# A prologue for the feed-forward stage of an adaptive-layer-norm transformer block with routed experts

## The chip, the core and the metric

The kernel runs on one core of a Trainium2 chip. The core has TensorE (PE), VectorE (DVE), ScalarE (ACT) and GpSimd (POOL), each with an instruction stream of its own, and SyncE (SP), which here issues transfers. Engines wait for one another through semaphores. An engine takes its instructions in the order in which they stand, so an instruction that waits holds up everything behind it. The metric is the device time of one execution in microseconds, the median of several.

## The reference

Input x has 16 batches of 256 tokens with 128 features. A conditioning vector per batch gives shift, scale and gate for two halves.

```
h = layernorm(x) * (1 + ca) + sa                 # per batch
n = rms(h) * ln1_w;  q, k, v = n@Wq, n@Wk, n@Wv  # 16 heads of 8, q and k normalised
p = softmax((q k^T + rel_bias[bucket]) * scale, strictly causal)
y = (p v) @ Wo + h
x = x + ga * (relu((rms(y) * ln2_w) @ W1) @ W2 + y)      # W1 128x512, W2 512x128
h = layernorm(x) * (1 + cb) + sb
s = sigmoid(h @ gate_w^T)                        # 32 experts
ids = top4(s + e_bias);  w = s[ids] / sum(s[ids])
x = x + gb * sum over the 4 experts e of w_e * ((silu(h@w1_e) * (h@w3_e)) @ w2_e)
```

All is float32.

## The kernel before

The kernel passes through four stages. A batch is two tiles of 128 tokens.

**Attention.** A loop over batches. For each of them PE makes scores for 8 units of two heads, DVE adds the bias (L1289), ACT takes the exponential (L703), PE multiplies by the values (`products`, L954). The last steps of batch b lie inside the sequence of batch b + 1: ACT brings the context out of PSUM (`context`, L710), PE transposes it (`ctx_T`, L970), DVE divides by the sum (`normalize`, L1308 and L1310), PE transposes and multiplies by Wo (`yn_T`, `y_out`), and DVE adds h and takes the statistics of y (`y_rows`, L1316 and L1320). For batch 15 these steps stand alone at the end.

**Feed-forward and routing.** The order is written by hand, engine by engine, as turns (`all_turns` and the four functions `turn`). Turn k does for a pair of batches the products of the feed-forward, for the pair before it the residual and the router's logits, and for the pair before that the choice of experts. So turns 0 and 1 fill this pipeline, turns 3 to 6 are a loop, and turns 8 and 9 drain it. The steps of one batch are:

- ACT copies y from the batch store (`stage`, L763), PE transposes it (`m_transposes`, L1040), ACT brings it out (`m_evac`, L767), PE makes the 512 hidden values (`hidden`, L1046), ACT applies relu (`relu`, L771), PE makes the second product (`mlp_out`, L1058).
- DVE scales that by the root of the RMS norm, adds y and x and takes statistics (`mlp_out` on DVE, L1477 to L1488). After a pair it takes their mean and root in 18 small instructions (`group_stats`, L324 to L1502).
- ACT normalises (`normal`, L780), DVE modulates (`modulated`, L1510 and L1512), PE transposes and makes the logits (`logits`, L1065 and L1069), ACT takes the tanh that gives the sigmoid (`routed`, L786 and L788) and copies the rows for the scatter (`copies`).
- DVE picks the four experts (`pick`, L1523 to L1553), PE counts the ranks (`ranks`, L1076), DVE makes the rows' positions (`place`, L1563 to L1569).
- POOL scatters the rows of the batch to HBM by 8 indirect transfers (L637), once the positions and the copies are there. Batches are scattered in order, through four sets of buffers. ACT's `normal` of batch b waits until the rows of batch b - 4 have been scattered.

Ahead of turn 0 DVE works out the roots for the RMS norm of all 32 tiles (L324 to L312, 18 instructions). After the last positions PE and DVE total the counts, SP writes 32 blocks of padding rows to HBM (L425), and waits for all scatters and for the padding before it loads the first sorted rows (L438).

**Experts.** 40 steps of four tiles of sorted rows, and then the sum over each token's four experts, the last stage.

## Time and profile before

| | |
|---|---|
| median of 3 runs | 689.37 us (688.49 to 689.84) |
| the profiled execution | 688.63 us, of which the span is 686.7 us |
| attention | to about 262 us of the span |
| feed-forward and routing | to 470.8 us, where the last scatter leaves POOL |
| experts and sum | from 472.4 us, the first load of sorted rows |
| busy, share of the span | PE 70%, DVE 66%, POOL 57%, ACT 46% |
| mean granted clock of PE | 0.862 |

The shares are means over stages with different limits. In the middle stage DVE is busy for 8 of every 10 us and POOL for 7 to 8, while PE has 2.4 to 8. A row of the timeline gives start, duration, engine, line, operation and operands, and in brackets how long the engine was idle before and what released it.

### The profile page before, as it was taken

The numbers are of one execution on the slowest core, as the hardware profiler recorded it, in microseconds if no ns is written. First come the engines' busy times: TensorE is split into PE (matmuls) and PEld (weight loads), VectorE is DVE, ScalarE is ACT, GpSimd is POOL, SyncE is SP. The second block draws the span as 40 slices with busy tenths as digits, with TensorE's granted clock in tenths as the row PEclk, the third lists the DMA queues.
The fourth block names the chain that finished last, engine by engine and source line by source line (L and its number), as shares of the span: only waits on it lengthen the run. The fifth ranks groups of instructions, "written<-read, shape, count | busy, mean of one in ns | idle before, by whom it ended". The sixth has DMA issues, their size and how long they took to land.

```text
span 686.7 us, 16134 instructions
## 1 busy us (share of the span) xinstructions
PE 481.4 (70%) x4426; PEld 371.9 (54%) x4427; DVE 454.3 (66%) x1486; ACT 315.2 (46%) x683; POOL 389.8 (57%) x606
## 2 busy tenths in 40 slices
PE   2568888888888776677766764222999999981057
PEld 0235555555555554565545553211899889980046
DVE  5776888888887774477786778850466666662028
ACT  0346777777787763432333323301566556430000
POOL 5565666666665400047676767773277777777700
PEclk9968999999999999977877876555999999995569
DMA  7996000000006006001111111145354545421178
GB/s 204 297 261 165 3 0 0 0 0 0 0 1 247 2 1 184 1 30 57 53 55 51 53 53 56 62 134 150 102 149 128 148 128 148 127 85 50 53 305 314
DMA packets 68850, 66.26 MB, mean 96 GB/s; under 512 B 8912, under 2 KB 60336, under 8 KB 68800
## 3 DMA queue, kind: packets, MB, share of 16 engines
q1 hardware_dynamic: 52096, 43.64, 21.5%
q0 software_dynamic: 8192, 17.84, 7.4%
q10 hardware_dynamic: 8512, 4.20, 2.1%
q8 instruction: 21, 0.34, 0.2%
q14 instruction: 29, 0.24, 0.1%
HBM read 40.86 MB, written 27.93 MB: 100 GB/s over the span
## 4 chain that ended last, share of the span: by engine, by line
DVE 26%; PE 25%; issue 22%; POOL 10%; DVEq 6%; ACT 6%; DMA 3%; POOLq 1%; SPq 1%; ACTq 0%
DVE L L1289 6%; PE PS L1046 5%; POOL xs L637 4%; POOL ys L655 3%; PE PS L931 3%; DVE yidx L1678 3%; PE PS L1137 2%; PE PS L1058 2%; PE PS L1206 2%; PE PS L906 2%; DVEq L335 2%; DVE YQ L1676 1%; PE PS L954 1%; POOL QKR L535 1%; PE PS L1069 1%
## 5 line engine op out<-in xcount | busy, mean ns | idle before, releaser
L637 POOL DMA_INDIRECT xs<-YQ,posi x128 | 124.9, 976 | 109.3 <-issue 98.3
L655 POOL DMA_INDIRECT ys<-YQ,yidx x128 | 122.6, 958 | 60.6 <-issue 34.2
L1289 DVE TENSOR_TENSOR L<-PS,BIAS 128x768 f32<-128x768 f32 x128 | 116.6, 952 | 39.0 <-PE PS L934 33.3
L703 ACT ACTIVATE PR<-L 128x768 f32<-128x768 f32 x128 | 106.0, 842 | 60.7 <-DVE L L1289 58.6
L1676 DVE SCALAR_TENSOR_TENSOR YQ<-PS,tag,YQ 128x128 f32 x160 | 56.2, 351 | 46.1 <-DVE yidx L1678 29.7
L1137 PE MATMUL PS<-BIAS,V 128*128 x320 | 64.1, 346 | 3.7 <-issue 1.6
L931 PE MATMUL PS<-YQ 32*128 32x256 f32 x512 | 47.3, 439 | 27.2 <-DVE L L1289 25.7
L1137 PEld LDWEIGHTS PS<-BIAS,V 128*128 128x128 f32 x320 | 53.0, 196 | 10.8 <-issue 10.8
L1046 PE MATMUL PS<-YT,w1s 128*128 128x256 f32 x128 | 42.3, 487 | 15.8 <-ACT YT L767 15.8
L1058 PE MATMUL PS<-w2s,hid 128*128 128x128 f32 x256 | 36.3, 300 | 14.5 <-ACT hid L771 14.5
L931 PEld LDWEIGHTS PS<-YQ 32*128 32x128 f32 x512 | 20.9, 188 | 46.8 <-DVE L L1289 33.1
L817 ACT ACTIVATE L<-PS 128x384 f32<-128x384 f32 x40 | 19.6, 491 | 54.9 <-PE PS L1137 53.6
L1206 PE MATMUL PS<-BIAS,ident 128*128 128x256 f32 x64 | 17.2, 424 | 39.3 <-DMA BIAS<-ys 38.9
L1058 PEld LDWEIGHTS PS<-w2s,hid 128*128 128x128 f32 x256 | 33.1, 209 | 19.2 <-ACT hid L771 17.9
L1046 PEld LDWEIGHTS PS<-YT,w1s 128*128 128x128 f32 x128 | 29.5, 242 | 25.2 <-ACT YT L767 20.4
L954 PE MATMUL PS<-PR,V 128*32 128x256 f32 x512 | 42.1, 400 | 1.4 <-DVE YQ L1316 1.1
L830 ACT ACTIVATE V<-PS 128x512 f32<-128x512 f32 x40 | 23.9, 597 | 33.2 <-PE PS L1129 33.2
L1129 PE MATMUL PS<-ident,PR 128*128 128x128 f32 x160 | 25.0, 281 | 18.3 <-DMA PR<-xs 18.3
L1206 PEld LDWEIGHTS PS<-BIAS,ident 128*128 128x128 f32 x64 | 13.2, 213 | 42.9 <-issue 40.9
L771 ACT ACTIVATE hid<-PS 128x1024 f32<-128x1024 f32 x16 | 16.4, 1023 | 43.7 <-PE PS L1046 43.7
L578 POOL TENSOR_SCALAR V<-RAW,rs 128x128 f32<-128x128 f32 x32 | 23.7, 749 | 22.1 <-issue 7.3
L906 PE MATMUL PS<-wqkv,hT 128*128 128x384 f32 x64 | 29.8, 596 | 6.6 <-DVE YQ L1276 4.3
(256 smaller groups left out, 1114.2 us busy)
## 6 DMA issues: line engine op xcount, KB each, us to landing
PR<-xs SPq DMA_DIRECT2D x160, 72.0 KB
BIAS<-ys SPq DMA_DIRECT2D x12, 512.0 KB, 8.2
modb<-mod_rows SPq DMA_DIRECT2D x1, 4096.0 KB, 14.0
dist_rep<-dist_row SPq DMA_DIRECT2D x4, 768.0 KB, 7.8
xs<-pad_row SPq DMA_DIRECT2D x33, 72.0 KB, 12.4
xs<-pad_row SPq DMA_DIRECT2D x1, 2304.0 KB, 17.8
X<-in_x ACTq DMA_DIRECT2D x4, 512.0 KB, 6.6
BIAS<-dist_rep SPq DMA_DIRECT2D x4, 512.0 KB, 8.6
```

The costliest lines, as they stand in the source:

```text
L637: pool.indirect_dma_start(out=xs, out_offset=bass.IndirectOffsetOnAxis(ap=posi[j][:, t * TOPK + k:t * TOPK + k + 1], axis=0), in_=ROWS[j][ ...
L655: pool.indirect_dma_start(out=ys, out_offset=bass.IndirectOffsetOnAxis(ap=yidx[:, n:n + 1], axis=0), in_=YQ[:, n * D:(n + 1) * D], in_offs ...
L703: act.activation(PR[u % 4][:, :], L[u % 2][:, :], ACT.Exp).then_inc(s["exp_done"], 1)
L906: last = pe.matmul(bank(PRE + t, 3 * D), hT[par][:, t * P:(t + 1) * P], wqkv[:, :], start=True, stop=True)
L931: pe.matmul(bank(S_A + quad, SEQ), KT[par][r, 0:P], QM[par][r, j, :], start=True, stop=True)
L954: pe.matmul(o, V[par][:, 0, h, :], pr[:, (j % 2) * HW:(j % 2) * HW + SEQ], start=True, stop=False, skip_group_check=True)
L1046: last = pe.matmul(bank(1 + ch // 2, SEQ, (ch % 2) * SEQ), w1s[:, ch * P:(ch + 1) * P], mT[n % 2], start=True, stop=True)
L1058: last = pe.matmul(bank(3 + 4 * (n % 2), P, t * P), hid[n % 2][:, ch, t * P:(t + 1) * P], w2s[:, ch, :], start=(ch == 0), stop=(ch == HID ...
L1137: last = pe.matmul(bank(2 + 2 * par + j // 2, 2 * INNER, (j % 2) * 2 * INNER), xgT[par][:, j * P:(j + 1) * P], w13[:, bass.ds(e * (2 * INN ...
L1206: last = pe.matmul(bank(n % 4, SEQ), ident[:, :], G[r][:, :, k, :], start=(k == 0), stop=(k == TOPK - 1))
L1289: return dve.tensor_tensor(L[u % 2][:, :].rearrange("p (j w) -> p j w", j=2), PS[:, at:at + 2, 0:HW], BIAS[:, u, :].rearrange("p (j w) -> ...
L1676: dve.scalar_tensor_tensor(to, bank(6 + par, D, k * D), tag[buf][:, k, 0:1], to, ALU.mult, ALU.add)
```

## The change

The two buffers for staged y and its transpose move from the context tile YT to the two RAW tiles of the attention, which are free once the last values and the last normalised q and k are made. So ACT can stage batches 0 and 1 inside the last attention sequence. The feed-forward's turns 0 and 1, and in turn 2 the choice of experts for batches 0 and 1 (on DVE all of turn 2), are replaced by a prologue in which batches 0 to 3 are handled one by one, and whose first products stand among the last context steps. The roots of the RMS norm are taken in two parts: tiles 0 to 29 ahead of the context steps of batch 15, and the last two at the end of turn 7. The turns from 3 on keep their order, except for that second part.

```diff
--- before.py
+++ after.py
-        mT = [YT[:, 2 * i, :] for i in range(2)]
-        YS = [YT[:, 2 * i + 1, :].rearrange("p (t d) -> p t d", t=TPB) for i in range(2)]
+        raw_flat = [RAW[i][:, :, :].rearrange("p t d -> p (t d)") for i in range(2)]
+        mT = [raw_flat[i][:, 0:SEQ] for i in range(2)]
+        YS = [raw_flat[i][:, SEQ:SEQ + TPB * D].rearrange("p (t d) -> p t d", t=TPB) for i in range(2)]
...
-        def all_turns(eng, turn):
+        def all_turns(eng, turn, entered=False):
...
-                turn(pair(k), pair(k - 1), pair(k - 2), pair(k + 1), k - 1, (k - 1) // 2)
-            for k in range(3):
-                one(k)
+                turn(pair(k), pair(k - 1), pair(k - 2) if k > 2 else [], pair(k + 1), k, (k - 1) // 2)
+            if not entered:
+                one(2)
...
+            def stage(b, n):
+                act.wait_ge(s["y_ready"], b + 1)
+                if not at(b, 0, 1):
+                    act.wait_ge(s["m_t"], b - 1)
+                act.activation(YS[n % 2], tok(Y, b, 0, TPB), ACT.Copy).then_inc(s["ys_staged"], 1)
...
+                if left == 0:
+                    act.wait_ge(s["v_ready"], NB)
+                    act.wait_ge(s["qn_done"], NB)
+                    stage(0, 0)
+                    stage(1, 1)
...
-            act.wait_ge(s["o2_done"], NB)
-            stage(0, 0)
-            stage(1, 1)
+            m_evac(0, 0)
+            context(NB - 1, 1)
+            relu(0, 0)
+            yn_T(NB - 1)
+            stage(2, 2)
+            m_evac(1, 1)
+            stage(3, 3)
+            normal(0, 0, 0, 0)
+            relu(1, 1)
+            routed(0, 0)
+            copies(0, 0)
+            m_evac(2, 2)
+            relu(2, 2)
+            m_evac(3, 3)
+            normal(1, 1, 1, 0)
+            routed(1, 1)
+            relu(3, 3)
+            copies(1, 1)
+            stage(4, 0)
+            stage(5, 1)
             all_turns(act, turn)
...
-            products(NB - 1, 1, 3)
-            ctx_T(NB - 1)
-            yn_T(NB - 1)
-            y_out(NB - 1)
-
-
-            pe.wait_ge(s["l_ready"], NB * UNITS + 2)
-            pe.wait_ge(s["w1_scaled"], 1)
...
+            pe.wait_ge(s["l_ready"], NB * UNITS + 1)
+            m_transposes(0, 0)
+            products(NB - 1, 1, 3)
+            pe.wait_ge(s["l_ready"], NB * UNITS + 2)
+            pe.wait_ge(s["w1_scaled"], 1)
+            hidden(0, 0)
+            ctx_T(NB - 1)
+            mlp_out(0, 0)
+            yn_T(NB - 1)
+            y_out(NB - 1)
+            m_transposes(1, 1)
+            hidden(1, 1)
+            logits(0, 0)
+            mlp_out(1, 1)
+            ranks(0, 0)
+            m_transposes(2, 2)
+            hidden(2, 2)
+            mlp_out(2, 2)
+            m_transposes(3, 3)
+            hidden(3, 3)
+            logits(1, 1)
+            mlp_out(3, 3)
+            ranks(1, 1)
             all_turns(pe, turn)
...
+            def y_roots(first, n):
+                r = slice(first, first + n)
+                mean_var(dve, st, r)
+                st.wait()
+                st(dve.tensor_tensor(st1[:, r], mean[:, r], mean[:, r], ALU.mult))
+                st.wait()
+                st(dve.scalar_tensor_tensor(var[:, r], st1[:, r], RMS_EPS, var[:, r], ALU.add, ALU.add))
+                st.wait()
+                rsqrt(dve, st, rstd[:, r], var[:, r], st1[:, r], st2[:, r])
+                st.wait()
+
+            y_roots(0, NT - TPB)
             normalize(NB - 1)
-            y_rows(NB - 1)
-
-
-            dve.wait_ge(s["y_ready"], NB)
-            mean_var(dve, st)
-            st.wait()
-            st(dve.tensor_tensor(st1[:, :], mean[:, :], mean[:, :], ALU.mult))
-            st.wait()
-            st(dve.scalar_tensor_tensor(var[:, :], st1[:, :], RMS_EPS, var[:, :], ALU.add, ALU.add))
-            st.wait()
-            rsqrt(dve, st, rstd[:, :], var[:, :], st1[:, :], st2[:, :])
-            st.wait()
             dve.wait_ge(s["ld_mod"], 16)
+            dve.wait_ge(s["h_scaled"], NB)
...
-                    group_stats(k, 2 * TPB)
+                    group_stats(k, 0, 2 * TPB)
...
+                if at(k, NPAIR - 1):
+                    y_roots(NT - TPB, TPB)
+
+            mlp_out(0, 0, 0)
+            group_stats(0, 0, TPB)
+            y_rows(NB - 1)
+            modulated(0, 0)
+            pick(0, 0)
+            place(0, 0)
+            mlp_out(1, 1, 1)
+            group_stats(1, TPB, TPB)
+            modulated(1, 1)
+            mlp_out(2, 2, 0)
+            pick(1, 1)
+            place(1, 1)
+            mlp_out(3, 3, 1)
+            group_stats(2, 0, 2 * TPB)
+            modulated(2, 2)
+            modulated(3, 3)
+            all_turns(dve, turn, entered=True)
```

POOL and SP keep their rows. **PE at the end of attention**, from the last products of batch 15. L954/L973 and L959/L978 are the products with the values, L970/L989 the transposes of the context, L976/L995 and L983/L1002 those of the normalised context and the product with Wo, L1040/L1050 the transposes of staged y, L1046/L1056 the hidden products, L1058/L1068 the second products. Before:

```order
L954 MATMUL PS<-PR,V 32x256 x4
L959 MATMUL PS<-PR,V 32x128 x4
L954 MATMUL PS<-PR,V 32x256 x4
L959 MATMUL PS<-PR,V 32x128 x4
L970 MATMUL PS<-ident,YT 128x128 x8
L976 MATMUL PS<-ident,YN 128x128 x2
L983 MATMUL PS<-wo,YNT 128x128 x2
L1040 MATMUL PS<-ident,YT 128x128 x2
L1046 MATMUL PS<-YT,w1s 128x256 x4
L1058 MATMUL PS<-w2s,hid 128x128 x8
```

After:

```order
L973 MATMUL PS<-PR,V 32x256 x4
L978 MATMUL PS<-PR,V 32x128 x4
L1050 MATMUL PS<-ident,RAW 128x128 x2
L973 MATMUL PS<-PR,V 32x256 x4
L978 MATMUL PS<-PR,V 32x128 x4
L1056 MATMUL PS<-RAW,w1s 128x256 x4
L989 MATMUL PS<-ident,YT 128x128 x8
L1068 MATMUL PS<-w2s,hid 128x128 x8
L995 MATMUL PS<-ident,YN 128x128 x2
L1002 MATMUL PS<-wo,YNT 128x128 x2
L1050 MATMUL PS<-ident,RAW 128x128 x2
L1056 MATMUL PS<-RAW,w1s 128x256 x4
```

The transposes and the hidden products of batch 0 now stand ahead of the context transposes, the second product of batch 0 ahead of those of the normalised context.

**DVE at the same place**, from the division of batch 15 on. Before, y and the statistics of batch 15 follow at once, then the roots of 32 tiles and the residuals of two batches:

```order
L1308 RECIPROCAL rden<-PS 128x32
L1310 TENSOR_TENSOR YN<-PS,rden 128x256
L1316 TENSOR_TENSOR YQ<-PS,YQ 128x256
L1320 BN_STATS stats<-YQ 128x6 x2
L324 TENSOR_TENSOR st<-stats 128x32
L325 TENSOR_TENSOR st<-stats 128x32
```

After, the roots of 30 tiles stand ahead of the division, and behind it the residual of batch 0 (L1511 to L1522) and its `group_stats`, which ends with nmr_g; then come y of batch 15, the modulation of batch 0 and its pick:

```order
L1537 SCALAR_TENSOR_TENSOR nmr_g<-mean_g,rstd_g 128x2
L1349 TENSOR_TENSOR YQ<-PS,YQ 128x256
L1353 BN_STATS stats<-YQ 128x6 x2
L1545 TENSOR_TENSOR YQ<-YQ,modb 128x2x128
L1547 TENSOR_TENSOR YQ<-YQ,modb 128x2x128
L1558 TENSOR_SCALAR score<-th 128x64
L1560 TENSOR_TENSOR sel<-score,ebias 128x64
L1564 MAX top<-sel 128x8 x2
```

Batch 0 is carried to its pick before the residual of batch 1 is taken.

**DVE at the end of turn 7**, from the positions of batch 11 on. Before, the pick of batch 12 follows the modulation of batch 13:

```order
L1567 TENSOR_REDUCE rk<-OHT 128x8
L1569 SCALAR_TENSOR_TENSOR posi<-nt,rk 128x8
L1510 TENSOR_TENSOR YQ<-YQ,modb 128x2x128
L1512 TENSOR_TENSOR YQ<-YQ,modb 128x2x128
L1523 TENSOR_SCALAR score<-th 128x64
L1525 TENSOR_TENSOR sel<-score,ebias 128x64
```

After, the 18 instructions of the second `y_roots` stand between them:

```order
L1604 SCALAR_TENSOR_TENSOR posi<-nt,rk 128x8
L1545 TENSOR_TENSOR YQ<-YQ,modb 128x2x128
L1547 TENSOR_TENSOR YQ<-YQ,modb 128x2x128
L325 TENSOR_TENSOR st<-stats 128x2
L326 TENSOR_TENSOR st<-stats 128x2
L327 TENSOR_TENSOR rstd<-stats 128x2
L329 TENSOR_SCALAR mean<-st 128x2
```

## Rows read from the trace of the kernel before

**Rows 1.** The page's costliest groups: line, engine, operation, count; busy, mean ns; idle before

```profile
L637 POOL DMA_INDIRECT xs<-YQ,posi x128 | 124.9, 976 | 109.3 <-issue 98.3
```

**Rows 2.** Waits between 297 and 471 us: who for whom, us, times, longest

```profile
POOL xs L637 <- DVE posi L1569: 10.9, 11, 1.3
```

**Rows 3.** Timeline of POOL (start, duration, engine, line, operation; idle before, releaser)

```profile
299.07 1.20 POOL L637 DMA_INDIRECT xs<-YQ,posi  x1 [62.49 <-issue]
...
420.11 0.95 POOL L637 DMA_INDIRECT xs<-YQ,posi  x1 [0.78 <-DVE posi L1569]
...
440.53 0.96 POOL L637 DMA_INDIRECT xs<-YQ,posi  x1 [0.30 <-issue]
...
469.81 0.96 POOL L637 DMA_INDIRECT xs<-YQ,posi  x1 [0.30 <-issue]
```

**Rows 4.** Timeline of DVE, the instruction that finishes a batch's positions

```profile
319.27 0.17 DVE L1569 SCALAR_TENSOR_TENSOR posi<-nt,rk 128x8 int32<-128x8 f32 x1
...
419.10 0.17 DVE L1569 SCALAR_TENSOR_TENSOR posi<-nt,rk 128x8 int32<-128x8 f32 x1
...
438.73 0.17 DVE L1569 SCALAR_TENSOR_TENSOR posi<-nt,rk 128x8 int32<-128x8 f32 x1
449.54 0.17 DVE L1569 SCALAR_TENSOR_TENSOR posi<-nt,rk 128x8 int32<-128x8 f32 x1
```

**Rows 5.** Timeline of SP's queue after the routing, and its waits there

```profile
451.68 18.68 SPq L425 DMA_DIRECT2D xs<-pad_row  x32
472.39 27.49 SPq L438 DMA_DIRECT2D PR<-xs  x40
...
SPq L442 <- DMA xs<-YQ,posi: 0.4, 1, 0.4
```

**Rows 6.** Timeline of DVE at the attention's end

```profile
261.92 0.36 DVE L1308 RECIPROCAL rden<-PS 128x32 f32<-128x32 f32 x1 [3.03 <-PE PS L970]
```

**Rows 7.** Timeline of all engines, the steps of the first batches

```profile
264.25 0.38 PE L1040 MATMUL PS<-ident,YT 128*128 128x128 f32 x2
265.11 1.99 PE L1046 MATMUL PS<-YT,w1s 128*128 128x256 f32 x8 [0.47 <-ACT YT L767]
268.22 2.05 PE L1058 MATMUL PS<-w2s,hid 128*128 128x128 f32 x16 [1.11 <-ACT hid L771]
270.43 0.61 DVE L1477 SCALAR_TENSOR_TENSOR XH<-PS,rstd,YQ 128x128 f32<-128x128 f32 x2 [1.22 <-PE PS L1058]
276.23 0.61 DVE L1477 SCALAR_TENSOR_TENSOR XH<-PS,rstd,YQ 128x128 f32<-128x128 f32 x2 [3.64 <-PE PS L1058]
278.42 0.17 DVE L324 TENSOR_TENSOR tg<-stats 128x4 f32<-128x4 f32 x1
281.41 0.16 DVE L1502 SCALAR_TENSOR_TENSOR nmr_g<-mean_g,rstd_g 128x4 f32<-128x4 f32 x1
285.61 1.64 ACT L780 ACTIVATE YQ<-X,nmr_g,rstd_g 128x128 f32<-128x128 f32 x4
286.51 0.43 DVE L1510 TENSOR_TENSOR YQ<-YQ,modb 128x256 f32<-128x256 f32 x1 [4.94 <-ACT YQ L780]
```

**Rows 8.** Timeline of DVE, first pick of experts and the end of turn 2

```profile
289.44 0.20 DVE L1523 TENSOR_SCALAR score<-th 128x64 f32<-128x64 f32 x1 [1.25 <-ACT th L788]
292.98 0.60 DVE L1477 SCALAR_TENSOR_TENSOR XH<-PS,rstd,YQ 128x128 f32<-128x128 f32 x2
...
309.56 0.42 DVE L1512 TENSOR_TENSOR YQ<-YQ,modb 128x256 f32<-128x256 f32 x1
```

**Rows 9.** Timeline of PE, products at the lower clock

```profile
313.83 3.78 PE L1046 MATMUL PS<-YT,w1s 128*128 128x256 f32 x8 [1.99 <-ACT YT L767]
318.80 3.77 PE L1058 MATMUL PS<-w2s,hid 128*128 128x128 f32 x16 [0.55 <-ACT hid L771]
```

**Rows 10.** A window: length, busy of the five, granted clock, DMA share, GB/s

```profile
290.00:294.00 4.00, 2.01 (x9) 1.59 (x10) 3.54 (x16) 2.15 (x6) 0.00 (x0) 0.71 0.00 0
```

**Rows 11.** Timeline of DVE, the pick of batch 12, after turn 7

```profile
420.85 0.20 DVE L1523 TENSOR_SCALAR score<-th 128x64 f32<-128x64 f32 x1 [0.79 <-ACT th L788]
```

More of the change, by code:

```diff
@@ L271, in one @@
             def one(k):
[L272 to L274 removed]
+                turn(pair(k), pair(k - 1), pair(k - 2) if k > 2 else [], pair(k + 1), k, (k - 1) // 2)
+            if not entered:
+                one(2)
             with eng.Fori(0, NPAIR // 2 - 2) as four:
                 b = four * 4
[L277 to L278 removed]
+                turn(pair_of(b + 6, 2), pair_of(b + 4, 0), pair_of(b + 2, 2), pair_of(b + 8, 0), four * 2 + 3, four + 1)
+                turn(pair_of(b + 8, 0), pair_of(b + 6, 2), pair_of(b + 4, 0), pair_of(b + 10, 2), four * 2 + 4, four + 1)
             for k in range(NPAIR - 1, NPAIR + 2):
@@ L754, in _ @@
                 sequence(NB - 1 - left, left % 2 ^ 1, left=left)
-            context(NB - 1, 1)
-            yn_T(NB - 1)
-            def stage(b, n):
-                act.wait_ge(s["y_ready"], b + 1)
-                if not at(b, 0, 1):
-                    act.wait_ge(s["m_t"], b - 1)
-                act.activation(YS[n % 2], tok(Y, b, 0, TPB), ACT.Copy).then_inc(s["ys_staged"], 1)
             def m_evac(b, n):
@@ L1590, in turn @@
                     modulated(*rows[1])
-            all_turns(dve, turn)
+                if at(k, NPAIR - 1):
[17 more added lines that the diff above has]
+            all_turns(dve, turn, entered=True)
             dve.wait_ge(s["cnt_pe"], 1)
```

30 lines of the change are left out of this document (14 added, 16 removed).

## The prediction

> **What bounds the kernel now.** I read the page first. Its slices show three regimes, and the change touches the seam between the first two and the order at the start of the second. The costliest group is POOL's scatter: 128 of them at a mean of 976 ns [rows 1]. So the first question is whether POOL sets the length of the middle stage. The timeline of POOL says that it runs from 299.07 to 470.77 [rows 3], 171.7 us. The last 24 scatters take 470.77 - 440.53 = 30.24 us, 1.26 us each, so 128 of them without a pause would take 161.5. The table of waits gives the difference: 11 times in this stage POOL waited for a batch's positions from DVE, 10.9 us in all [rows 2]. The last of these waits is at batch 11, whose positions are done at 419.27 [rows 4] and whose first scatter starts at 420.11 [rows 3], 0.84 us later. From there POOL has no more pause. So the chain that ends the stage is: DVE's turns up to the positions of batch 11, and then 40 scatters of POOL. An earlier first scatter alone is worth nothing; an earlier DVE is worth what it brings at batch 11, as long as the batches behind it keep up.
>
> A second chain ends close behind. After the last positions, at 449.71 [rows 4], SP is released and writes the padding from 451.68 to 470.36. It then reads its tables, and stood before its wait for the scatters 0.4 us before the last of them landed; the first load went out at 472.39 [rows 5]. So if the scatters ended earlier and the padding did not, only 0.4 us would be gained.
>
> **The start of the stage, before.** At the end of attention DVE waits 3.03 us for the context transposes, until 261.92 [rows 6]. The first residual starts at 270.43, the second at 276.23, after a wait of 3.64 us for PE; its statistics end at 281.57, and then DVE waits 4.94 us until 286.51, because ACT takes its normalisation, at 285.61, only behind the relus of batches 2 and 3 [rows 7]. The first pick starts at 289.44 [rows 8]. The pipeline is entered when the modulation of batch 3 ends, at 309.98 [rows 8]; the loop starts there.
>
> **The steps of a batch.** Durations at the full clock, all from [rows 7] and [rows 8]. Transposes of y and their copy out: 265.11 - 264.25 = 0.86. Hidden products 1.99. Relu with its hops 268.22 - 267.10 = 1.12. Second products 2.05. A round of all this on PE takes 5.8 (276.23 - 270.43). Residual 278.42 - 276.23 = 2.19. Statistics of a group 281.57 - 278.42 = 3.15, for 18 instructions. Normalisation 1.64 / 4 x 2 = 0.82 a batch. Modulation 0.88. From there to a usable tanh 289.44 - 287.39 = 2.05. Pick 292.98 - 289.44 = 3.54. Positions about 1.1.
>
> **Part 1, the first products among the context steps.** PE's transposes of batch 0 fit ahead of the last exponential, but the hidden products stand ahead of the context transposes. These need their copy by ACT anyway, so I charge 1.99 less some 0.6: the division comes at about 263.3 and not 261.9. Bounds are 0 (all beside the copy) and 1.99. The first roots of 30 tiles, 18 instructions like those of the group statistics, so at least 3.15 us, lie in DVE's wait of 3.03 + 1.4; if the wait were gone, they would cost these 3 us, as they do now behind the statistics of batch 15. In return the residual of batch 0 needs hidden products from about 260.1 (the context transposes' place: 261.92 less a copy and eight transposes, estimated 1.8), 1.99 + 1.12 + 2.05, so it starts at 265.4 and not 270.43. ACT's two staging copies lie in its idle time before an exponential, and the two RAW tiles have no reader left. I take both as free.
>
> **Part 2, batches 0 to 3 one by one.** I follow the engines' orders by hand.
> - DVE: residual and statistics of batch 0 to 270.8. ACT's normalisation to 271.6, y of batch 15 beside it, modulation to 272.7, tanh 274.8, pick to 278.3, positions 279.4. The first scatter could leave at 280.4, 18.6 us earlier than now.
> - Then residual 1 and its own statistics (a second run of 18 instructions, 3.15 us that did not exist) to 284.8, normalisation and modulation 286.5, residual 2 to 288.7, pick 1 to 292.2, positions 293.3, residual 3 and statistics to 298.6.
> - PE is behind this, not ahead: the relu of batch 3 stands on ACT behind the tanh of batch 1 (288.6), so it ends at 289.6, the second products of batch 3 at 291.7, ranks of batch 1 to 292.3. Only then come the transposes of batch 4. Batch 5's relu ends at 292.3 + 0.86 + 5.8 + 1.99 + 1.1 = 302.1, and ACT has the normalisation of batches 2 and 3 behind it. So DVE waits from 298.6 to 303.0, and the modulation of batch 3 ends at 303.0 + 0.8 + 0.88 = 304.7.
>
> That is 5.3 us earlier than 309.98. I take 4.7 at the positions of batch 2 (now 319.27, [rows 4]), since the clock's falls lie otherwise and the first tanh of the loop comes late. Bounds: 6 with PE at its full clock throughout, 3 with one batch more at the lower one (hidden products 3.78 for 1.99, second ones 3.77 for 2.05 [rows 9], 3.5 a batch, part of it in waits). The loop is the same code on all engines, and DVE bounds it, so 4.7 arrives at batch 11. The 18.6 us at the first scatter do not: they become POOL's pauses at batches 1 and 2.
>
> **Part 3, the second roots.** They are 18 more small instructions at the end of turn 7. The nearest row is the group statistics, 3.15 us [rows 7]. DVE waits 0.79 us for the tanh of batch 12 at this place [rows 11], so 2.4 reach the pick. Bounds: 3.15, if the tanh comes no later, and 1.5. The positions of batches 12 to 15 are thus earlier by only 4.7 - 2.4 = 2.3. Those of batch 13, at 438.90 [rows 4], would be at 436.6, and 0.84 later, at 437.4, its scatters can start, now 440.53 [rows 3]. POOL is then without pause again. So the last scatter is 3.1 earlier.
>
> **Part 4, the padding.** The last positions are 2.3 earlier, and so are SP's 18.68 us of padding. SP has lost 0.4 of waiting at most, so the first load is at 472.39 - 2.3 - 0.4 = 469.7. By the scatters it would be 469.3. The padding becomes the last, and the stage ends 2.7 us earlier. Bounds 0.7 (loop 3 earlier, roots 2.7) and 5 (loop 6, roots 1.5, rounded up).
>
> **The sum.** Parts 1 and 2 bring -4.7 at the loop's entry, the second roots +2.4, SP's margin before the scatters' landing -0.4: -2.7. The profiled execution has a span of 686.7 and takes 688.63; 1.9 lies around the span and stays. It would become 685.9. The median is 689.37, 0.74 more, so I predict 686.7.
>
> **The clock as a rival, and the slower side.** In the window 290 to 294 the granted clock of PE fell from 1.00 to 0.50, mean 0.71, after PE had been busy for little of the stretch, 2.01 of 4 us with nine matmuls [rows 10]; there are two levels, 2.4 and 1.2 GHz. Before the change turns 0 and 1 run wholly at the upper one. In the prologue PE is more often idle, for some 3 us before the logits of batch 0 above all, so I expect one fall near 274. If the clock then stays low until batch 5's relu, batches 2 to 5 cost 3.5 us more each. PE waits for ACT or DVE for some 4 us in that stretch, so 14 - 4 = 10 us reach the loop, which enters 5 later than now, and with the second roots the stage ends 7 later: about 696. It decides from the point at which the prologue loses more than 2.7, one batch at the lower clock beyond my count. Against it: in the whole stage the page's slices show the clock fall and come back again and again, with a mean of 5 tenths only where PE has almost nothing to do, and in the prologue PE has the products of a batch every 12 us or faster. The skill speaks for it: the Trainium skill, "TensorE: Matmul & The Clock Gate", Part 1, holds that the low clock is the rule and "activity releases the throttle", so a sparse prologue would be throttled more than the dense turns that it replaces. The fall in rows 10 agrees; that the low clock lasts through the prologue no row shows. I give the slower side 0.08.
>
> **Other rivals.**
> - The gain is spent before the end (0.18). The loop enters only 2 to 3.5 earlier, the roots cost 2.4 to 3, and the padding hides the rest: 0 to 1.4 gained, 688.0 to 689.4. For it: three terms of 2 to 5 us are differenced. Against it: the order by hand leaves DVE idle for only 4.4 us before the loop, where it idles some 13 now (3.03 + 1.22 + 3.64 + 4.94).
> - The second roots are covered and the scatters decide (0.14): if the tanh of batch 12 comes later than now, or the padding lands sooner, the gain is 3.5 to 5, 684.4 to 685.9.
> - POOL was the bound all along (0.02): the 18.6 us pass through, 670.8. The 11 waits speak against it.
>
> The forecast itself, 1.4 to 3.5 gained, gets 0.58. What a measurement here can tell from no change is 0.2%, 1.4 us. Faster: 0.58 + 0.14 + 0.02 = 0.74; the same 0.18; slower 0.08. The range from 684.6 to 689.4 leaves out the slow clock, POOL and the edges of the others.
>
> **What the profile after would show.** The first scatter near 280 and a pause of POOL at batches 1 and 2; a DVE wait of about 4 us before the modulation of batch 2; the positions of batch 2 near 314.6; those of batch 11 near 414.4 and of batch 15 near 447.2; a POOL wait at batch 13; SP's first load near 469.7 with no wait for scatters. I am wrong if the positions of batch 2 are later than 317, or if the load waits for scatters that end after the padding.

## The result, and the profile after

The changed kernel takes 686.21 us (median of 5 runs, 685.09 to 687.61) where the kernel before took 689.84 in 5 runs of the same session. The ratio is 0.9951, with a 95% interval from 0.9938 to 0.9964: 3.4 us faster, with an interval of 2.5 to 4.3. The forecast was 686.7. The profiled execution took 686.9 with a span of 685.0, against 688.63 and 686.7. That pair differs by only 1.7: the profile of before was one of its quicker runs and that of after one of its slower ones.

For comparing profiles I need a common start. The last pair but one of DVE's additions to the scores is the same in all kernels, a row with a wait of 1.44 for PE. I call its start the mark. Here it is, first in the kernel before, then in the changed one:

```profile
253.04 1.82 DVE L1289 TENSOR_TENSOR L<-PS,BIAS 128x768 f32<-128x768 f32 x2 [1.44 <-PE PS L934]
```

```profile
254.02 1.82 DVE L1322 TENSOR_TENSOR L<-PS,BIAS 128x768 f32<-128x768 f32 x2 [1.44 <-PE PS L953]
```

The attention ahead of it took 1.0 us longer in that execution of the changed kernel. Over all my profiles the mark lies between 251.9 and 254.6.

DVE in the changed kernel, from the timeline (columns as in [rows 3 and 4]):

```profile
264.42 0.36 DVE L1341 RECIPROCAL rden<-PS 128x32 f32<-128x32 f32 x1 [0.83 <-PE PS L989]
266.76 0.61 DVE L1511 SCALAR_TENSOR_TENSOR XH<-PS,rstd,YQ 128x128 f32<-128x128 f32 x2 [1.52 <-PE PS L1068]
...
275.79 0.19 DVE L1558 TENSOR_SCALAR score<-th 128x64 f32<-128x64 f32 x1 [1.89 <-ACT th L790]
280.24 0.17 DVE L1604 SCALAR_TENSOR_TENSOR posi<-nt,rk 128x8 int32<-128x8 f32 x1
...
303.59 0.42 DVE L1545 TENSOR_TENSOR YQ<-YQ,modb 128x256 f32<-128x256 f32 x1 [3.62 <-ACT YQ L782]
315.09 0.17 DVE L1604 SCALAR_TENSOR_TENSOR posi<-nt,rk 128x8 int32<-128x8 f32 x1
...
405.59 0.17 DVE L1604 SCALAR_TENSOR_TENSOR posi<-nt,rk 128x8 int32<-128x8 f32 x1
416.40 0.17 DVE L1604 SCALAR_TENSOR_TENSOR posi<-nt,rk 128x8 int32<-128x8 f32 x1
427.54 0.17 DVE L1604 SCALAR_TENSOR_TENSOR posi<-nt,rk 128x8 int32<-128x8 f32 x1
...
449.12 0.17 DVE L1604 SCALAR_TENSOR_TENSOR posi<-nt,rk 128x8 int32<-128x8 f32 x1
```

Take 1.0 off each for the late mark and lay them beside [rows 4, 6, 7]: the prologue runs as it was worked out, within half a microsecond at every step. The wait of 3.62 at the modulation of batch 2 is the one that was forecast as about 4. Counted from the mark, the positions of batch 2 come at 61.07 instead of 66.23, 5.2 us earlier. But those of batch 11 are only 3.7 earlier, and those of batch 15 only 1.4.

POOL and SP at the same places (compare [rows 3, 5]); the last column of the SP rows is the number of transfers:

```profile
281.43 1.20 POOL L638 DMA_INDIRECT xs<-YQ,posi  x1 [43.87 <-issue]
295.48 0.97 POOL L638 DMA_INDIRECT xs<-YQ,posi  x1 [4.00 <-DVE posi L1604]
316.10 1.17 POOL L638 DMA_INDIRECT xs<-YQ,posi  x1 [10.79 <-DVE posi L1604]
...
428.54 0.97 POOL L638 DMA_INDIRECT xs<-YQ,posi  x1 [1.10 <-DVE posi L1604]
...
468.64 0.96 POOL L638 DMA_INDIRECT xs<-YQ,posi  x1 [0.30 <-issue]
```

```profile
451.22 18.82 SPq L426 DMA_DIRECT2D xs<-pad_row  x32
471.73 26.75 SPq L439 DMA_DIRECT2D PR<-xs  x40
```

Counted from the mark, the first scatter is 18.6 us earlier and the last only 2.2: POOL waits 26.9 us for positions now, 10.9 before [rows 2]. The padding ends last, and SP no longer waits for scatters. The first load of sorted rows goes out 217.71 behind the mark instead of 219.35, so 1.6 us of the gain are seen there in this pair of profiles. What lies outside that stretch differs from one execution to the next in any kernel: the mark by up to 2.6 us, and the time from the first load to the end of the span (214.3 before, 213.3 after) between 213.3 and 215.2.

### The profile page after: what moved, and what is told of

It reads as the page before. It is cut to its first block, busy times and chain, and to the rows that moved or that the text cites. A ratio compares the mean times of both kernels' runs of the same rounds, so it can differ in the third digit from the quotient of the medians.

```text
span 685.0 us, 16172 instructions
## 1 busy us (share of the span) xinstructions
PE 474.9 (69%) x4426; PEld 367.0 (54%) x4427; DVE 458.8 (67%) x1522; ACT 315.6 (46%) x683; POOL 390.4 (57%) x606
## 4 chain that ended last, share of the span: by engine, by line
DVE 31%; issue 24%; PE 20%; DVEq 6%; POOL 6%; ACT 6%; SPq 3%; DMA 3%; POOLq 1%; ACTq 0%
DVE L L1322 6%; PE PS L1056 4%; POOL ys L656 4%; DVE yidx L1732 3%; PE PS L950 2%; PE PS L1068 2%; PE PS L1239 2%; SPq L426 2%; DVEq L336 2%; POOL QKR L536 2%; ACT YT L711 2%; DVE YQ L1730 1%; PE PS L1170 1%; PE PS L1079 1%; DVEq L1730 1%
## 5 line engine op out<-in xcount | busy, mean ns | idle before, releaser
L1056 PE MATMUL PS<-RAW,w1s 128*128 128x256 f32 x128 | 40.4, 470 | 13.8 <-ACT RAW L769 13.8
L1068 PE MATMUL PS<-w2s,hid 128*128 128x128 f32 x256 | 34.4, 290 | 13.0 <-ACT hid L773 13.0
L973 PE MATMUL PS<-PR,V 128*32 128x256 f32 x512 | 41.7, 396 | 1.4 <-DVE YQ L1349 1.1
L1056 PEld LDWEIGHTS PS<-RAW,w1s 128*128 128x128 f32 x128 | 28.4, 234 | 22.6 <-ACT RAW L769 18.0
L1068 PEld LDWEIGHTS PS<-w2s,hid 128*128 128x128 f32 x256 | 31.3, 200 | 17.1 <-ACT hid L773 15.7
```

Source lines behind the costliest of these rows:

```text
L973: pe.matmul(o, V[par][:, 0, h, :], pr[:, (j % 2) * HW:(j % 2) * HW + SEQ], start=True, stop=False, skip_group_check=True)
L1056: last = pe.matmul(bank(1 + ch // 2, SEQ, (ch % 2) * SEQ), w1s[:, ch * P:(ch + 1) * P], mT[n % 2], start=True, stop=True)
L1068: last = pe.matmul(bank(3 + 4 * (n % 2), P, t * P), hid[n % 2][:, ch, t * P:(t + 1) * P], w2s[:, ch, :], start=(ch == 0), stop=(ch == HID ...
```

## The experiments

All are timed in five rounds beside the kernel before; ratios are to it, with 95% intervals. What settles most of them is a table worked out from the profiles: the time from the mark to the positions of batch 2 (the entry), from there to those of batch 10 (the loop), and on to those of batch 15 (the end). The first three columns come from one profile each, the ratio from all executions.

```
kernel                        entry   loop    end   ratio   (interval)
before                        66.23  89.02  41.25
staging alone                 66.22  88.94  41.27  1.0006  (0.9994 to 1.0018)
before, more roots            66.22  88.89  43.36  1.0008  (0.9996 to 1.0020)
before, written out           66.23  86.71  40.18  0.9945  (0.9925 to 0.9965)
seam alone                    62.96  88.83  40.22  0.9934  (0.9915 to 0.9953)
seam alone, written out       62.98  86.74  40.16  0.9898  (0.9878 to 0.9918)
after (the change)            61.07  90.50  43.53  0.9951  (0.9938 to 0.9964)
after, roots in the wait      60.96  88.86  40.10  0.9907  (0.9893 to 0.9922)
  the same, written out       61.10  86.54  40.58  0.9894  (0.9875 to 0.9912)
after, roots in both          63.31  88.77  43.68  0.9951  (0.9934 to 0.9968)
after, scatter held           63.47  90.39  43.53  0.9961  (0.9949 to 0.9973)
after, PE kept busy           62.39  89.88  43.55  0.9947  (0.9929 to 0.9965)
after, written out            63.97  86.51  43.35  0.9911  (0.9891 to 0.9930)
after, seam apart             69.42  89.82  43.51  1.0099  (1.0070 to 1.0128)
```

### The second roots in DVE's wait

```
             group_stats(2, 0, 2 * TPB)
+            y_roots(NT - TPB, TPB)
             modulated(2, 2)
...
-                if at(k, NPAIR - 1):
-                    y_roots(NT - TPB, TPB)
```

> The changed kernel with the second roots (18 small DVE instructions for the last two tiles) taken from the end of turn 7 and put between the statistics of batches 2 and 3 and the modulation of batch 2, where DVE waited 3.62 us. My theory (Part 3 of the prediction): the roots cost about 2.3 us in front of the pick of batch 12 and nothing in the wait. Then the modulation of batch 2 still starts at about 303.6 with no or a short wait, batches 12 to 15 are 2.3 earlier (positions of batch 15 near 446.8 instead of 449.1), the padding ends 2.3 earlier, but then the scatters decide: batch 11 starts them at about 417.3, 40 scatters take 50.4, so the first load goes out near 470.0 instead of 471.7: a gain of 1.7 us, 684.5 (683.9 to 685.3). Rival 1: the tanh of batch 12 comes late enough that turn 7 waits for it anyway: positions of batch 15 move by under 0.8, gain under 0.6. Rival 2: the roots fill more than the wait at the entry and push everything by their excess: the modulation of batch 2 starts later than 304, no gain or a loss.

Measured: 683.07, ratio 0.9907. Its DVE and SP rows:

```profile
303.16 0.42 DVE L1545 TENSOR_TENSOR YQ<-YQ,modb 128x256 f32<-128x256 f32 x1 [0.42 <-ACT YQ L782]
...
414.15 0.17 DVE L1604 SCALAR_TENSOR_TENSOR posi<-nt,rk 128x8 int32<-128x8 f32 x1
422.07 0.17 DVE L1604 SCALAR_TENSOR_TENSOR posi<-nt,rk 128x8 int32<-128x8 f32 x1
```

```profile
445.54 19.13 SPq L426 DMA_DIRECT2D xs<-pad_row  x32
467.25 32.60 SPq L439 DMA_DIRECT2D PR<-xs  x46
```

The modulation of batch 2 still waits 0.42, so the roots are free there. From batch 11 to 12 takes 7.92 us instead of 11.14: against this kernel the second roots cost 3.2 in turn 7, not the 2.3 I expected. The gain of 3 us over the changed kernel is larger than 1.7; the loop, too, is shorter, 88.86 for 90.50. Later experiments follow that.

### The roots added to the kernel before

```
                 if rows:
                     modulated(*rows[1])
+                if at(k, NPAIR - 2):
+                    y_roots(NT - TPB, TPB)
```

> The kernel before with the roots of the last two tiles worked out a second time at the end of the turn in which the changed kernel has them (18 small DVE instructions behind the modulation of batch 11). Nothing else changes. It measures Part 3 by itself. My theory: 3.15 us of instructions, less the wait of 0.79 for the tanh of batch 12 that they cover: positions of batches 12 to 15 come 2.4 later, the padding is last, 691.7 (691.1 to 692.4). Rival: the kernel with them in the wait showed 3.2 between the same two positions; if the tanh comes early whatever stands there, the cost is 3.2: 692.5 or more. Third: POOL's scatters decide the end: then 1.6 or less, since POOL had 0.8 of wait left at batch 11 only.

Measured: 690.39, ratio 1.0008. The table shows 2.1 more at the end (43.36 for 41.25). The kernel before and the one with the staging alone are the odd ones: without roots there, every other kernel takes 40.1 to 40.6 on this stretch. The tanh of batch 12 in the kernel before:

```profile
420.60 0.22 ACT L788 ACTIVATE th<-PS 128x64 f32<-128x64 f32 x1 [1.15 <-PE PS L1069]
```

ACT waited 1.15 for the logits, which PE computed at the lower clock (granted 0.50 from 418 to 420 us); in four of the five kernels with the shorter end it waits 0.72, with PE at the upper clock, and the fifth (the roots in the wait, written out) has 1.15 and the longest of those ends, 40.58. So the wait of 0.79 in [rows 11], which I took off the price, goes with PE's clock at that place. It stood in both profiles that have this order of turns and no roots there. At the first load the profile shows 1.8 us more than before (221.10 behind the mark for 219.35), because before it the scatters ended last and now the padding does. The time rose by only 0.5 us (interval -0.3 to 1.4). Where the rest went is open.

### The scatters held back

```
+            pool.wait_ge(s["pos_ready"], 2)
             with pool.Fori(0, NB // GROUP) as g:
```

> The changed kernel with one more wait on POOL: the first scatter is held until the positions of batch 1 are there, so it starts near 295.3 and not at 281.4. My theory (Part 2): the early first scatter is worth nothing, since POOL pauses 26.9 us for positions behind it; 16 scatters take 20.2, so the ones of batch 2 still start at about 316 (positions at 315.1). Time as after, 686.2 within 0.6. Rival: POOL's own length decides somewhere behind (scatters landing later in the first group hold ACT's normalisation of batches 4 and 5, or POOL is not again waiting by batch 11): 2 to 14 us slower.

Measured: 686.88, ratio 0.9961, against 0.9951: as after.

```profile
296.03 1.29 POOL L638 DMA_INDIRECT xs<-YQ,posi  x1 [60.43 <-issue]
...
327.88 0.95 POOL L638 DMA_INDIRECT xs<-YQ,posi  x1 [1.32 <-DVE posi L1605]
...
468.97 0.96 POOL L638 DMA_INDIRECT xs<-YQ,posi  x1 [0.31 <-issue]
```

The first scatter is 14.6 us later, POOL waits for positions again at batch 3, and the last scatter is 0.3 later. (Counted from the mark it is 16.6 and 2.3; the 2.3 are the longer entry in the table, 63.47 for 61.07. That goes with PE's clock and not with the hold: the modulation of batch 1, which needs no scatter, already waits 3.02 for 0.95, and kernels without the hold show the same.) The early scatters are worth nothing that the time could show.

### The staging alone

```
-            act.wait_ge(s["o2_done"], NB)
-            stage(0, 0)
-            stage(1, 1)
...
+                if left == 0:
...
+                    stage(0, 0)
+                    stage(1, 1)
```

(with the raw buffers for the staged tiles, as in the change; the rest is the kernel before)

> The kernel before with the staging alone: staged y and its transposes lie in the raw buffers and ACT copies batches 0 and 1 among the exponentials of batch 15 instead of behind the last context copy; the turns, their order and the roots are as before. My theory: the transposes of batch 0 already followed the output product of attention without a wait, so nothing is gained by the staging itself: 689.8 within 0.7 (0 to 0.3 us of PE's sequence at most). Rival: the copies among the exponentials delay the last context (slower by 0.7), or free ACT at the seam by 0.7 us and bring that (faster by 0.7).

Measured: 689.61, ratio 1.0006; the entry takes 66.22, as before. The staging is worth nothing by itself and only makes room for what follows.

### The seam undone, and the seam alone

The first puts batch 0's transposes and products back behind the last context steps in the changed kernel, on PE as shown (lines that wait are left out) and on ACT likewise:

```
-            m_transposes(0, 0)
             products(NB - 1, 1, 3)
-            hidden(0, 0)
             ctx_T(NB - 1)
-            mlp_out(0, 0)
             yn_T(NB - 1)
             y_out(NB - 1)
+            m_transposes(0, 0)
+            hidden(0, 0)
+            mlp_out(0, 0)
```

> The changed kernel with the last context steps undone from the first products on PE and ACT: products of the last context, context transposes, transposes of y, output product, and only then the transposes, hidden and second products of batch 0; on ACT both context copies ahead of the copy and relu of batch 0. DVE, the staging and the order of batches 0 to 3 stay. My theory: the division is about 1.5 earlier (262.9), but the residual of batch 0 starts at about 271.2 instead of 266.8, and since DVE is the chain of the prologue, every step up to the entry of the loop is 4 to 6 later (modulation of batch 3 ends near 310, as in the kernel before); with the second roots still in turn 7 the stage ends later than in the kernel before: 691.5 (690 to 693), slower than after by 4.5 to 6 and than before by 1.5 to 3. Rival: the gain of the change comes from handling the batches singly and not from the order at the seam: then it stays within 1.5 of after (686 to 687.7).

Measured: 694.88, ratio 1.0099: 6.8 us slower than before (4.8 to 8.8), beyond the expected band. Its rows, of DVE and of PE:

```profile
273.45 0.61 DVE L1510 SCALAR_TENSOR_TENSOR XH<-PS,rstd,YQ 128x128 f32<-128x128 f32 x2 [10.21 <-PE PS L1068]
```

```profile
264.23 1.22 PE L1002 MATMUL PS<-wo,YNT 128*128 128x128 f32 x4 [0.47 <-ACT YNT L717]
265.24 0.64 PE L1050 MATMUL PS<-ident,RAW 128*128 128x128 f32 x2
266.35 3.78 PE L1056 MATMUL PS<-RAW,w1s 128*128 128x256 f32 x8 [0.47 <-ACT RAW L769]
```

DVE stands 10.2 us before the first residual. Most of my miss there is the clock: the output product, the transposes and the hidden products of batch 0 ran at the lower level (granted 0.50 from 264 to 270 us; 3.78 where 1.99 was usual), behind two microseconds, 262 to 264, in which PE was busy for 0.47. Single handling without the seam is worse than no change.

The second is the other half: the kernel before with the staging and the seam, DVE's code as it was, the batches in pairs, all roots in one piece. On PE (waits left out; ACT likewise):

```
+            m_transposes(0, 0)
             products(NB - 1, 1, 3)
+            hidden(0, 0)
             ctx_T(NB - 1)
+            mlp_out(0, 0)
             yn_T(NB - 1)
             y_out(NB - 1)
+            m_transposes(1, 1)
+            hidden(1, 1)
+            mlp_out(1, 1)
-            all_turns(pe, turn)
+            all_turns(pe, turn, 1)
```

> The kernel before with the seam alone: raw buffers for the staging, batches 0 and 1 staged among the last exponentials, transposes and products of batch 0 among the last context steps on PE and ACT, those of batch 1 right behind the output product. DVE is as before: all roots behind the statistics of batch 15, batches handled in pairs from the first turn, no second roots. My theory: hidden products ahead of the context transposes put the division and with it the roots and residual 0 about 1.1 later (271.5), but residual 1 no longer waits for PE (273.7 instead of 276.2), the relus of batches 2 and 3 and so the first normalisation come 3.5 earlier, and the modulation of batch 3 ends near 306.3 instead of 310.0. With no second roots to pay, positions 15 are 3.5 earlier than before (446.0) and the time is about 686.0 (685.0 to 687.5), no worse than the whole change. Rival: what brings the gain is the single handling (statistics and tanh of batch 0 early); then this stays within 1.2 of before (688.1 to 689.5).

Measured: 684.99, ratio 0.9934, the level of the whole change or a little better, and a little better than I expected.

```profile
271.62 0.61 DVE L1489 SCALAR_TENSOR_TENSOR XH<-PS,rstd,YQ 128x128 f32<-128x128 f32 x2
273.82 0.61 DVE L1489 SCALAR_TENSOR_TENSOR XH<-PS,rstd,YQ 128x128 f32<-128x128 f32 x2
283.04 0.42 DVE L1522 TENSOR_TENSOR YQ<-YQ,modb 128x256 f32<-128x256 f32 x1 [3.88 <-ACT YQ L782]
...
294.40 0.17 DVE L1581 SCALAR_TENSOR_TENSOR posi<-nt,rk 128x8 int32<-128x8 f32 x1
```

Both residuals start without a wait, as expected (compare 270.43 and 276.23 in [rows 7]). The entry takes 62.96, 3.3 less than before; 1.0 more comes at the end (40.22 for 41.25), where the wait for the late tanh of batch 12 is gone. So the reordering at the seam is what pays. Handling the batches singly buys at most 2 us more at the entry and costs 3.3 at the end with the second roots in turn 7 (43.53 for 40.22). With those roots in the wait it costs nothing there, but whether it then gains can't be told: 0.9907 and 0.9934 have intervals that meet.

### A stall at the loop's jump back

In the changed kernel's trace something stood in turn 5, the second pass of DVE's loop. First ACT's tanh of batch 6, then DVE's rows around the jump:

```profile
350.32 0.22 ACT L790 ACTIVATE th<-PS 128x64 f32<-128x64 f32 x1 [1.15 <-PE PS L1079]
```

```profile
349.51 0.42 DVE L1547 TENSOR_TENSOR YQ<-YQ,modb 128x256 f32<-128x256 f32 x1
352.66 0.19 DVE L1558 TENSOR_SCALAR score<-th 128x64 f32<-128x64 f32 x1 [2.72 <-ACT th L790]
...
354.88 0.20 DVE L1569 FIND_INDEX8 topi<-top,sel 128x8 uint32<-128x32 f32 x1 [0.93 <-issue]
```

The tanh is done at 350.54, the pick starts at 352.66, and inside it DVE stands 0.93 with no releaser. With the roots in the wait it starts 0.25 behind the tanh. Two experiments write the loop of turns 3 to 6 out on DVE alone, in the changed kernel and in the one with the roots in the wait (the other engines keep the loop):

```
-            with eng.Fori(0, NPAIR // 2 - 2) as four:
+            for k in range(3, NPAIR - 1):
+                one(k)
```

> The changed kernel with DVE's loop over turns 3 to 6 written out, the other engines as they are. In the changed kernel's trace DVE started the pick of batch 6, the first instruction behind its loop's jump back, 2.1 us after its tanh was ready, and stood 0.93 more inside it with no releaser; in the kernel before it started at once. Theory: a stall of DVE's instruction supply at the jump back, 3 us, of which 0.7 to 1.5 reach the positions behind it (the rest lies in the wait for the ranks). Written out, pick 6 starts within 0.3 of its tanh, positions of batch 11 are near 415.3 and the time is 685.2 (684.2 to 686.0). Rival: the late start has to do with ACT or a semaphore and not with the jump: no change (686.2 within 0.5). Second rival: longer straight code meets the same stall at other places: same or up to 3 slower.

> The kernel with the second roots in the wait at the loop's entry, and DVE's loop written out. That kernel showed no late start at the jump back (pick 6 came 0.64 after the work before it, 0.25 after its tanh). By the theory of the stall nothing is to be gained here: 683.1 within 0.6. If the written-out code itself were faster or slower (no loop overhead, more code to bring in), it would show here as a difference of more than 0.8.

Measured: 684.13 (0.9911) and 682.92 (0.9894). The pick of batch 6 starts on time in both, but the loop also took 2.3 us less where no stall had been (86.54 for 88.86), although the time of that kernel hardly shows it (0.9894 for 0.9907, intervals that overlap). So two things were mixed, and a control on the kernel before parts them.

> The kernel before with DVE's loop written out, a control for the changed kernel with the same edit, which gained 2.7 us on it. Two causes are mixed there. From the positions of batch 2 to those of batch 10 took 89.0 us in the kernel before, 90.5 in the changed one, 88.9 with the second roots in the wait, and 86.5 in both written-out kernels. Theory: the loop form costs 2.4 us in any kernel (88.9 to 86.5), and the late start at the jump back 1.5 more, in the changed kernel alone. Then this control goes from 89.0 to 86.5 between the two positions, and is faster than before by 2 to 2.5: 687.5 (686.9 to 688.2). Rival: all of the 2.7 is the stall at the jump, and the loop form costs nothing in itself: 689.7 within 0.6.

Measured: 684.92, ratio 0.9945, and 86.71 in the loop: as the theory had it. In time 3.8 were gained, interval 2.4 to 5.2, more than the 2.0 to 2.5 expected; at the first load the profile shows 2.1 (217.25 behind the mark for 219.35), since the scatters end last there. The same residual of batch 7, first with the loop, then written out:

```profile
341.46 0.61 DVE L1477 SCALAR_TENSOR_TENSOR XH<-PS,rstd,YQ 128x128 f32<-128x128 f32 x2
342.22 0.43 DVE L1481 TENSOR_TENSOR XH<-XH,modb 128x256 f32<-128x256 f32 x1
342.77 0.43 DVE L1484 TENSOR_TENSOR X<-X,XH 128x256 f32 x1
```

```profile
342.56 0.60 DVE L1481 SCALAR_TENSOR_TENSOR XH<-PS,rstd,YQ 128x128 f32<-128x128 f32 x2
343.19 0.42 DVE L1485 TENSOR_TENSOR XH<-XH,modb 128x256 f32<-128x256 f32 x1
343.65 0.42 DVE L1488 TENSOR_TENSOR X<-X,XH 128x256 f32<-128x256 f32 x1
```

These instructions last as long, but their starts lie 0.76 and 0.55 apart with addresses from the loop's counter and 0.63 and 0.46 with fixed ones. The steps of `group_stats` behind them, whose tiles have fixed addresses in both, mostly keep their distance of 0.20; but two of them (L328 and L329) last 0.40 and 0.32 with the loop and 0.17 and 0.16 written out. So what is shown is the price of the loop's form. Addresses from the counter may be part of it, and the semaphore values waited for are made from the counter too; nothing here separates them.

The stall itself was tested by moving the loop in the code: the roots worked out twice, ahead of the loop and behind it.

```
             group_stats(2, 0, 2 * TPB)
+            y_roots(NT - TPB, TPB)
             modulated(2, 2)
```

> The changed kernel with the roots of the last two tiles worked out twice, in the wait at the loop's entry and again at the end of turn 7. The work in front of batch 12 is that of the changed kernel; what differs is that 18 instructions more stand ahead of DVE's loop. Theory of instruction supply: the late start at the jump back (2.1 and 0.9 us) depends on where the loop's code lies and not on what it does, so it goes away here as in the kernel with these roots in the wait alone: positions 2 to 10 take 88.9 and not 90.4, time 684.8 (684.0 to 685.8), and the remaining 1.7 to that kernel is the price of the roots in turn 7. Rival: the late start comes from the roots that stand behind the loop: then it stays, 686.2 within 0.7.

Measured: the loop takes 88.77 and the late start is gone, as the theory of instruction supply had it. The time, 685.95 with a ratio of 0.9951, does not show the 1.4 expected; its twelve runs spread from 683.5 to 688.6, and in the profiled one the prologue met a longer low clock (entry 63.31). The DMA view of 300 to 420 us has the last piece, the queue that brings instructions (packets, MB, share), first in the changed kernel, then in the one with the roots in the wait:

```profile
q14 instruction: 9, 0.07, 0.2%
```

```profile
q14 instruction: 4, 0.03, 0.1%
```

The four kernels with the late start (the change, scatters held, PE kept busy, seam apart) have 9 packets there; the other ten have 4 or 5. Two of the nine fall into the 5 us of the stall, 350 to 355, where the kernel with the roots in the wait has none:

```profile
q14 instruction: 2, 0.02, 1.3%
```

The Trainium skill, "Runtime: NRT & Kernel Launch", "Instruction fetch mechanics", says it: a taken branch whose target lies outside the two pages at hand makes the engine wait for a DMA of the target page. The trace agrees with it, packets and late start together; where the loop's code lies in those pages no run here shows.

How much of the stall reaches the positions is seen in the step from batch 5 to 6. Its two ends, in the kernel before and in the changed one:

```profile
352.63 0.17 DVE L1569 SCALAR_TENSOR_TENSOR posi<-nt,rk 128x8 int32<-128x8 f32 x1
...
363.70 0.17 DVE L1569 SCALAR_TENSOR_TENSOR posi<-nt,rk 128x8 int32<-128x8 f32 x1
```

```profile
348.82 0.17 DVE L1604 SCALAR_TENSOR_TENSOR posi<-nt,rk 128x8 int32<-128x8 f32 x1
...
360.74 0.17 DVE L1604 SCALAR_TENSOR_TENSOR posi<-nt,rk 128x8 int32<-128x8 f32 x1
```

That is 11.92 for 11.07, 0.85 more. The four kernels with the stall take 11.8 to 11.9 for it, the six others that keep the loop 10.5 to 11.2.

### PE kept busy

```
             hidden(1, 1)
+            idle_products(10)
             logits(0, 0)
...
             logits(1, 1)
+            idle_products(4)
             mlp_out(3, 3)
```

> The changed kernel with 14 products more on PE whose results nobody reads (128x256, 0.25 us each at the full clock): ten behind the hidden products of batch 1, where PE waited 3.3 us for the modulation of batch 0, four ahead of the second products of batch 3, where it waited 1.2. They are there to keep the granted clock up in the prologue. In the profiled run of the changed kernel the clock fell once near 276 and came back after 3.4 us; in two of its relatives it fell long enough to reach hidden products behind it (3.78 for 1.99), and DVE waited 4.0 and 6.0 at the modulation of batch 2 instead of 3.6. Theory: second products of batch 1 take 2.05 instead of 3.46, DVE's wait at the modulation of batch 2 is at most 3.7, and the loop is entered up to 2 earlier in the executions that were hit: 685.5 (684.5 to 686.2). Rival: PE's time there is off the path, or the falls come back in the loop: 686.2 within 0.5. Second rival: the extra products delay the logits of batch 0: slower by up to 1.

Measured: 686.42, ratio 0.9947: no change.

```profile
269.24 4.48 PE L1120 MATMUL PS<-RAW,w1s 128*128 128x256 f32 x20
273.55 0.38 PE L1075 MATMUL PS<-ident,YQ 128*128 128x128 f32 x2
274.88 2.03 PE L1068 MATMUL PS<-w2s,hid 128*128 128x128 f32 x16
```

The clock stayed up (2.03, where the changed kernel had 3.46 at 275.33), but each product takes two instructions (20 for the ten) and about twice what I had counted, so the ten took 4.5 us and pushed the logits of batch 0 back. Counted from the mark the logits of batch 0 start 0.9 later. The entry, 62.39, is worse than the 61.07 of the execution without them. Whether a right-sized dose would help stays open.

### The seam alone, written out

This is the kernel with the seam alone and the edit of DVE's loop from above.

> The kernel with the seam alone (batches in pairs, all roots at once) and DVE's loop written out: the candidate without any of the single handling. Positions 2 to 10 took 88.8 with the loop; at 86.5 the padding and the scatters both end 2.3 earlier, as long as POOL keeps a pause at batch 11 (0.77 there now, and 10.08 a batch against DVE's 10.8). From 685.0 to 682.7 (682.0 to 683.6), equal to the changed kernel with the roots in the wait and the loop written out (682.9). Rival: POOL, which starts 14 us later here, becomes the bound: 684.0 or more.

Measured: 682.13, ratio 0.9898, as expected and the lowest median of all: 1.0% below the kernel before and, by the ratios, 0.5% below the changed one, with no single handling in it. The roots in the wait, written out (0.9894), cannot be told from it.

## Why the prediction was right, and where it was not

- **The bound.** Right: DVE's turns decide, and an early scatter is worth nothing (scatters held). The padding is last in the changed kernel. With a shorter end the scatters come last again: with the roots in the wait the last one leaves POOL at 465.64, 1.0 us behind the padding, and the first load goes out 2.6 us behind the padding, where it was 1.7.
- **Part 1.** Right in size: residual 0 at 265.8 from the mark of before (265.4 forecast), the division at 263.4 (263.3). The staging is free, as taken.
- **Part 2.** Right, at the good end of a spread that the working did not have. The loop's entry was taken as 4.7 earlier and came 5.2 earlier in the profiled execution. In the six other kernels with the same order at the seam and single handling the entry took 61.0 to 64.0, so it came 2.3 to 5.3 earlier. The three long ones without extra products on PE (63.3 to 64.0) have hidden products at the lower clock, and the short ones have none. This row is of the changed kernel written out, where DVE then waited 6.01:

```profile
293.07 3.78 PE L1060 MATMUL PS<-RAW,w1s 128*128 128x256 f32 x8 [0.47 <-ACT RAW L773]
```

- **"So 4.7 arrives at batch 11."** This step failed: of the 5.2 at the entry, 3.7 arrived. Same code on all engines did not mean the same time. 1.5 us were lost between batches 2 and 10 (90.50 for 89.02). Of these, 0.85 lie in the step with the stall at the jump back, which comes and goes with the code ahead of the loop and which no row of before showed. The other 0.6 lie in the steps from batch 3 to 4 and from 7 to 8, where nothing jumps; other kernels with this loop differ there as much, and the cause is open.
- **Part 3.** Right for this pair: 2.4 was put, and the end took 2.3 more (43.53 for 41.25), 2.1 in the control on the kernel before. It rests on the late tanh of the kernel before. Against kernels without that wait the same roots cost 3.2 to 3.6 (the upper bound had been 3.15), and 2.8 against the one with them in the wait, written out, where 0.54 of the wait stands. The last wait of POOL came at batch 12 and not at batch 13, as was forecast.
- **Part 4.** Right: the padding ends last, no wait for scatters.
- **The sum.** From the mark, the positions of batch 15 come 1.4 earlier, not 2.3, and the first load 1.6 earlier, not 2.7; the loop is what makes the difference. The time came out 3.4 lower (2.5 to 4.3). So the number was hit by more than the chain that was worked out: 0.9 to 2.7 us of the gain lie where this pair of profiles does not show them, and a longer entry in other executions would make the gap larger. That the forecast of 2.7 is near 3.4 is in this part luck; where the rest is gained stays open.
- **The clock as a rival.** Its strong form did not come. A weak form did: 2 to 3 us at the entry in three of the six profiles of this order without extra products. The singly handled prologue is more exposed to it: with the batches in pairs the entry is the same within 0.02 in all six profiles, before the seam's change (66.22, 66.23) and after it (62.96, 62.98).
- **What was missed.** Which part of the change pays. The working credited the prologue as a whole; the seam alone brings 4.6 us (3.2 to 5.9), and the single handling with its roots in turn 7 brings nothing more.

## What to carry to other kernels

Fill the bubbles of a seam first, by letting the next stage's first products run among the last stage's small steps; that alone may be the whole gain. A piece of work that can be done at any time, such as these roots, goes into a wait that stands in the profile: there they cost nothing, on the chain 2.1 to 3.6 us. And count an edit's effect on the code behind it: the number of instructions ahead of a loop decided here whether its jump back stalled. Last, look at which stretch of the profile a gain lies in before the sum is called confirmed: here the time agreed better with the forecast than the stretch did that the forecast was about.

## What the runs showed of the hardware

- After the jump back of DVE's loop the first instruction of the changed kernel came 2.1 us late and another 0.9 late, with 9 packets instead of 4 on the instruction queue q14. Four of the kernels show it, and the step from batch 5 to 6 took 0.6 to 0.9 us more there than in five of the six kernels that keep the loop without the stall. 18 more small instructions ahead of the loop made it go away.
- In DVE's loop, instructions with addresses from the counter start 0.1 us further apart than the same ones written out: 2.1 to 2.3 us over four turns in three pairs of kernels without the stall, of which the addresses need not be all.
- 18 small DVE instructions in a chain took 3.15 us on 128x2 (from the first start to the last end, below), as long as on 128x4 in [rows 7].

```profile
417.28 0.15 DVE L325 TENSOR_TENSOR st<-stats 128x2 f32<-128x2 f32 x1
...
420.27 0.16 DVE L313 SCALAR_TENSOR_TENSOR rstd<-st,rstd 128x2 f32<-128x2 f32 x1
```
